# A mixture-of-experts tail where TensorE, not GpSimd, adds the two expert results of each token

## The chip, the cores and the metric

The kernel runs on one core of one Trainium2 chip. The metric is the device time of one execution in microseconds (us). Three executions of the kernel before took 910.62, 911.58 and 914.34 us (median 911.58). All data is float32 and one core does all the work.

## What is computed

Input x is 8 sequences of 1024 tokens of 128 numbers. Two blocks follow each other, each with a residual and a layernorm around it: a Mamba-2 mixer with a small MLP, and a mixture of 8 experts, of which each token takes two. Only the end of the second block matters here:

```python
probs = jax.nn.softmax(x @ Wr + br, axis=-1)
gates, ids = jax.lax.top_k(probs, K)                       # K = 2
...
h = jax.nn.silu(jnp.einsum('ecd,edh->ech', xg, W1) + b1[:, None, :])
out = jnp.einsum('ech,ehd->ecd', h, W2) + b2[:, None, :]
gated = out * disp_g.reshape(E, cap, 1)
y = jnp.zeros((N, Dm), x.dtype).at[disp_tok].add(gated.reshape(E * cap, Dm))
...
x = x + _layernorm(_L0_ffn_ref(...), axis=-1)
```

So every token has up to two gated expert results. They are added, the sum is normalised over its 128 numbers, and x (after the first block) is added.

## The kernel before

The program is written engine by engine; each engine has its own instruction list and they meet at semaphores (`need(engine, sem, t)` waits until step t of a producer is done, and its last argument allows so many steps of lead). Stages follow one another: normalisation, the mixer, the MLP, routing, and the last stage, in which the experts run and the results are combined. The change touches only that last stage.

**Experts.** 80 columns of 128 slots are cut into 24 pieces of 2 to 4 columns. For each piece GpSimd issues indirect DMAs that fetch the token rows (`fetch`, L1863), TensorE turns them (`turn`, L1888), multiplies them into `pH` (`up`, L1897, four banks) and `pO` (`down`, L1905), and turns them back into `pB` (`back`, L1913). ScalarE applies silu (L1928) and the output bias (L1935), VectorE scales by the gate (`results`, L1977), and GpSimd issues the indirect DMAs (`leave`, L1871) that scatter the rows into the DRAM tensor `choice`, first choices in its one half, second choices in the other. All eight PSUM banks belong to this stage: `pT` two, `pH` four, `pO` and `pB` one each.

**Combining.** When all scatters have landed, the 64 tiles of 128 tokens are gone through in 19 groups: 14 of 4 tiles, three of 2, two of 1 (`widths`). SyncE's queue loads for each group the first results into `ys` (L1846) and the second into `yb` (L1847), both SBUF; nine groups are loaded ahead, and from then on each store of group g (L1851) stands in front of the loads of group g+9. GpSimd waits for both loads and adds yb to ys in place (`both`, L1879). Then:

- VectorE, `moments` (L1985): one bn_stats for each tile of the sum;
- VectorE, `combined` (L1991): one bn_aggr for each tile;
- ScalarE, `rooted` (L1944): the square root of the variances;
- VectorE, `inverse` (L1997 and L1999): reciprocal and shift;
- ScalarE, `normal` (L1950): scale and shift, one activation for each tile, ys in place;
- VectorE, `add_x1` (L2004): one add of x over the group; then the store.

The order on VectorE is written out by hand: in iteration g it does moments of g, inverse of g-1, combined of g and add_x1 of g-2. ScalarE does the root of g and then the normalisation of g-1.

```python
in_turn(GROUPS, [(0, moments), (1, inverse), (0, combined), (2, add_x1)])   # VectorE
in_turn(GROUPS, [(0, rooted), (1, normal)])                                 # ScalarE
in_turn(GROUPS, [(0, load), (8, store)])                                    # SyncE
```

TensorE has nothing to do once the experts' last piece is turned back. At the kernel's start (L326, in `idle`) and at the start of the MLP (L1346) it is given products of ones with zeros that nobody reads.

Of the kernel before, what the change touches and what calls it, by code (L numbers as in the profile page):

```python
# [27 lines left out]
ALU = mybir.AluOpType  # L28
ACT = mybir.ActivationFunctionType
# [3 lines left out]
SEQS, LEN, D = 8, 1024, 128  # L33
# [25 lines left out]
def need(eng, sem, t, back=0):  # L59

    value = t + 1 - back
    if not isinstance(value, int) or value > 0:
        eng.wait_ge(sem, value)
# [33 lines left out]
def build(nc, x, ln_w, ln_b, in_proj_w, conv_w, conv_b, dt_bias, A_log, D_skip, rms_w, out_proj_w,  # L97
# [4 lines left out]
    with ExitStack() as ctx:  # L102
# [8 lines left out]
        def sem(name):  # L111
            s = nc.alloc_semaphore(name=name)
            stage_sems.append(s)
            return s
# [8 lines left out]
        ident = sb("ident", [P, P])  # L123
        ones = sb("ones", [P, P])
# [4 lines left out]
        zrow = sb("zrow", [P, 8 * D])  # L129
# [45 lines left out]
        with ExitStack() as st:  # L175
# [5 lines left out]
            def pst(name, shape):  # L181
                return st.enter_context(nc.psum_tensor(name, shape, F32))
# [18 lines left out]
            pT = [pst(f"n_pT{k}", [P, 2, 512]) for k in range(2)]  # L201
# [934 lines left out]
        with ExitStack() as st:  # L1136
            st.callback(stage_over)
            NB, G = 4, 2
            GROUPS, N = TILES // G, G * P
# [602 lines left out]
        with ExitStack() as st:  # L1742
# [4 lines left out]
            TOTAL = len(sizes)  # L1747
# [42 lines left out]
            def of_group(g):  # L1790
                return slice(first_tile[g], first_tile[g + 1])
# [5 lines left out]
            def in_turn(steps, stages):  # L1797

                for i in range(steps + max(lag for lag, _ in stages)):
                    for lag, stage in stages:  # L1800
                        if 0 <= i - lag < steps:
                            stage(i - lag)
            pT = [pst("e_pT0"), pst("e_pT1")]
            pH = [pst(f"e_pH{c}") for c in range(NF)]
            pO, pB = pst("e_pO"), pst("e_pB")
            s_we = [sem("e_we0"), sem("e_we1")]
            s_xg = [sem(f"e_xg{k}") for k in range(RING)]
            s_scat = [sem(f"e_scat{k}") for k in range(RING)]
# [46 lines left out]
            @block.gpsimd  # L1855
            def _(g):
                def fetch(n):
                    need(g, s_pt, n, RING)
                    need(g, s_g1, n, RING)
                    need(g, s_g2, n, RING)  # L1860
                    for i in range(sizes[n]):
                        c = starts[n] + i
                        g.indirect_dma_start(xg[:, n % RING, i, :], None, table,  # L1863
                                             bass.IndirectOffsetOnAxis(ap=token_of[:, c:c + 1], axis=0),
                                             bounds_check=TOKENS - 1, oob_is_err=False).then_inc(s_xg[n % RING], 16)

                def leave(n):
                    need(g, s_yo, n)
                    for i in range(sizes[n]):
                        c = starts[n] + i  # L1870
                        g.indirect_dma_start(choice, bass.IndirectOffsetOnAxis(ap=choice_of[:, c:c + 1], axis=0),  # L1871
                                             yo[:, n % RING, i, :], None, bounds_check=2 * TOKENS - 1,
                                             oob_is_err=False).then_inc(s_scat[n % RING], 16)
                g.wait_ge(filled, 16 * FILLS)
                staged([(0, fetch), (LAG, leave)])

                def both(n):
                    g.wait_ge(s_in[n], 32)
                    g.tensor_tensor(ys[:, of_group(n)], ys[:, of_group(n)], yb[:, of_group(n)], ALU.add).then_inc(s_ys2, 1)  # L1879
                in_turn(GROUPS, [(0, both)])  # L1880

            @block.tensor
            def _(pe):
                def turn(n):
# [32 lines left out]
                pe.wait_ge(s_bias, 1)  # L1917
                staged([(2, up), (3, down), (4, back), (0, turn)])

            @block.scalar  # L1920
            def _(a):
                def silus(n):
                    need(a, s_po, n, 2)
                    w = P * sizes[n]
                    for c in range(NF):
                        f = NF * expert(n) + c
                        need(a, s_ph, NF * n + c)
                        a.activation(hb[:, n % 2, c, 0:w], pH[c][:, 0:w], ACT.Silu, bias=bcols[:, f:f + 1]).then_inc(s_h, 1)  # L1928

                def outs(n):  # L1930
                    need(a, s_po, n)
                    need(a, s_pb, n, 2)
                    w = P * sizes[n]
                    f = EXPERTS * NF + expert(n)
                    a.activation(oT[:, n % 2, 0:w], pO[:, 0:w], ACT.Identity, bias=bcols[:, f:f + 1]).then_inc(s_o, 1)  # L1935
                a.wait_ge(s_turned, 1)
                a.activation(bcols[:, :], pB[:, 0:NR], ACT.Copy).then_inc(s_bias, 1)
                a.wait_ge(s_bias, 1)
                staged([(2, silus), (3, outs)])

                def rooted(g):
                    need(a, s_var, g)
                    w = widths[g]
                    a.activation(c_sd[:, g, 0:w], c_mv[:, g, 0:w, 1], ACT.Sqrt, bias=eps[:, 0:1]).then_inc(s_sd, 1)  # L1944

                def normal(g):
                    need(a, s_sh, g)
                    for i in range(widths[g]):
                        t = first_tile[g] + i
                        ins = a.activation(ys[:, t, :], ys[:, t, :], ACT.Identity, bias=c_sh[:, g, i:i + 1], scale=c_rs[:, g, i:i + 1])  # L1950
                    ins.then_inc(s_yna, 1)
                in_turn(GROUPS, [(0, rooted), (1, normal)])

            @block.vector
            def _(v):
                def gates_of(n):
                    k, w = n % RING, sizes[n]
                    arrived(v, n)
                    need(v, s_yo, n, RING)
                    v.tensor_tensor(g1[:, k, 0:w], xg[:, k, 0:w, D], is_first[:, columns(n)], ALU.mult).then_inc(s_g1, 1)  # L1960
                    v.tensor_tensor(g2[:, k, 0:w], xg[:, k, 0:w, D + 1], is_other[:, columns(n)], ALU.mult).then_inc(s_g2, 1)
                    need(v, s_g1, n)
                    need(v, s_g2, n)
                    v.tensor_tensor(gate[:, k, 0:w], g1[:, k, 0:w], g2[:, k, 0:w], ALU.add).then_inc(s_gate, 1)

                def fetched(n):
                    need(v, s_pt, n)
                    need(v, s_ph, NF * n + NF - 1, 3 * NF)
                    v.tensor_copy(xgT[:, n % 3, 0:P * sizes[n]], pT[n % 2][:, 0:P * sizes[n]]).then_inc(s_xgT, 1)  # L1969

                def results(n):
                    k, w = n % RING, sizes[n]
                    need(v, s_pb, n)
                    if n >= RING:
                        v.wait_ge(s_scat[k], 16 * blocks_upto(n - RING))
                    need(v, s_gate, n)
                    v.tensor_tensor(yo[:, k, 0:w, :], pB[:, 0:P * w].rearrange("p (i d) -> p i d", d=D),  # L1977
                                    gate[:, k, 0:w].unsqueeze(2).broadcast_to([P, w, D]), ALU.mult).then_inc(s_yo, 1)
                staged([(4, results), (0, fetched), (0, gates_of)])

                def moments(g):
                    need(v, s_var, g, 2)
                    need(v, s_ys2, g)
                    for i in range(widths[g]):
                        ins = v.bn_stats(c_st[:, g % 2, i, :], ys[:, first_tile[g] + i, :])  # L1985
                    ins.then_inc(s_st, 1)

                def combined(g):
                    need(v, s_st, g)
                    for i in range(widths[g]):  # L1990
                        ins = v.bn_aggr(c_mv[:, g, i, :], c_st[:, g % 2, i, :])  # L1991
                    ins.then_inc(s_var, 1)

                def inverse(g):
                    need(v, s_sd, g)
                    w = widths[g]
                    v.reciprocal(c_rs[:, g, 0:w], c_sd[:, g, 0:w]).then_inc(s_rs, 1)  # L1997
                    need(v, s_rs, g)
                    v.scalar_tensor_tensor(out=c_sh[:, g, 0:w], in0=c_mv[:, g, 0:w, 0], scalar=-1.0, in1=c_rs[:, g, 0:w],  # L1999
                                           op0=ALU.mult, op1=ALU.mult).then_inc(s_sh, 1)  # L2000

                def add_x1(g):
                    need(v, s_yna, g)
                    v.tensor_tensor(ys[:, of_group(g)], ys[:, of_group(g)], x1[:, of_group(g), :], ALU.add).then_inc(s_ot, 1)  # L2004
                in_turn(GROUPS, [(0, moments), (1, inverse), (0, combined), (2, add_x1)])


# [22 lines left out]
```

## Time and profile before

| | |
|---|---|
| median of three runs (lowest, highest) | 911.58 us (910.62, 914.34) |
| the profiled execution's own time | 916.2 us |
| its span, first to last instruction | 914.5 us |
| mean granted TensorE clock | 0.847 of full |
| TensorE / VectorE / ScalarE / GpSimd busy | 686.5 / 611.7 / 490.2 / 463.9 us |
| first load of the combining issued | 865.09 us into the span |

The times in rows of the trace are microseconds from the span's start. The median is the number to compare with; durations come from the one profiled execution. A granted clock of 1.00 is TensorE at 2.4 GHz, 0.50 at 1.2 GHz.

### The profile page before, as it was taken

How to read it: one execution, taken by the hardware profiler on the slowest of the kernel's cores; microseconds unless marked ns; L12 is line 12 of the kernel's file. 1: busy time of each engine (PE TensorE's matmuls, PEld its weight loads, DVE VectorE, ACT ScalarE, POOL GpSimd, SP SyncE). 2: the span in 40 equal slices, each digit the busy share in tenths (PEclk: the TensorE clock that was granted, in tenths of full speed). 3: DMA queues.
4: the chain of work that ended last, by engine and by line, in shares of the span. 5: the costliest groups of instructions: out<-in, count | busy, mean ns of one | idle time of the engine just before them, and what ended most of it. 6: DMA issues, size and time to landing. Idle time of an engine off the chain costs nothing. (4 is left out here: it accounts for less than half of the span.)

```text
span 914.5 us, 14429 instructions
## 1 busy us (share of the span) xinstructions
PE 686.5 (75%) x3774; PEld 479.3 (52%) x3774; DVE 611.7 (67%) x2161; ACT 490.2 (54%) x1207; POOL 463.9 (51%) x594
## 2 busy tenths in 40 slices
PE   7558999999999997999998311374977877888200
PEld 3325677777777765989897211242434433444100
DVE  7957999999999955899898687891111111111088
ACT  4874666667667765878775145151422332234157
POOL 7514676667666762334333500006567666765572
PEclk8867999999999999999999555555999878898755
DMA  8930000000000006000000040003212221221295
GB/s 211 394 115 1 1 1 2 1 1 2 1 2 1 1 2 170 16 2 1 2 1 1 1 187 0 0 0 89 60 40 72 67 62 42 72 65 39 69 347 171
DMA packets 50413, 52.91 MB, mean 58 GB/s; under 512 B 7576, under 2 KB 39624, under 8 KB 50080
## 3 DMA queue, kind: packets, MB, share of 16 engines
q1 hardware_dynamic: 44496, 41.62, 14.0%
q0 software_dynamic: 5120, 10.37, 4.3%
q8 instruction: 29, 0.48, 0.2%
q14 instruction: 48, 0.39, 0.2%
q10 hardware_dynamic: 720, 0.05, 0.1%
HBM read 28.04 MB, written 24.18 MB: 57 GB/s over the span
## 5 line engine op out<-in xcount | busy, mean ns | idle before, releaser
L888 DVE SCALAR_TENSOR_TENSOR s_cv<-s_pU,tap_w,s_cv 128x256 f32<-128x256 f32 x372 | 153.5, 477 | 12.3 <-ACT s_cv L819 12.0
L1863 POOL DMA_INDIRECT arena<-token_rows,token_of x80 | 81.3, 1017 | 118.3 <-issue 118.0
L1977 DVE TENSOR_TENSOR arena<-e_pB,e_gate 128x384 f32<-128x384 f32 (+2 forms) x24 | 14.5, 603 | 151.7 <-remote 106.4
L1871 POOL DMA_INDIRECT choice_rows<-arena,choice_of x80 | 79.6, 996 | 58.4 <-DVE arena L1977 37.0
L1928 ACT ACTIVATE e_h<-e_pH,e_bcols 128x384 f32<-128x384 f32 (+2 forms) x96 | 56.5, 618 | 91.6 <-remote 59.0
L1897 PE MATMUL e_pH<-e_xgT,e_w 128*128 128x384 f32 (+2 forms) x192 | 90.5, 605 | 14.7 <-issue 13.8
L1905 PE MATMUL e_pO<-e_h,e_w 128*128 128x384 f32 (+2 forms) x192 | 80.7, 568 | 7.9 <-ACT e_oT L1935 6.4
L687 POOL TENSOR_TENSOR s_xa<-s_xt,arena 128x512 f32<-128x512 f32 x32 | 34.4, 1076 | 88.4 <-ACT s_xt L837 88.4
L819 ACT ACTIVATE s_cv<-s_pU,tap_b,tap_w 128x256 f32<-128x256 f32 x124 | 63.7, 561 | 23.4 <-PE s_pU L721 23.0
L721 PE MATMUL s_pU<-arena,w_in 128*128 128x262 f32 x248 | 69.3, 403 | 7.7 <-DVE s_cv L888 3.4
L1905 PEld LDWEIGHTS e_pO<-e_h,e_w 128*128 128x128 f32 x192 | 39.7, 210 | 47.7 <-issue 37.1
L1897 PEld LDWEIGHTS e_pH<-e_xgT,e_w 128*128 128x128 f32 x192 | 36.9, 212 | 51.7 <-issue 37.4
L1370 PE MATMUL m_pM<-w_m,m_h 128*128 128x128 f32 x512 | 63.9, 279 | 0.1
L1361 PE MATMUL m_pH<-m_hT,w_m 128*128 128x256 f32 x256 | 60.7, 380 | 2.1 <-ACT m_h L1244 1.5
L1370 PEld LDWEIGHTS m_pM<-w_m,m_h 128*128 128x128 f32 x512 | 61.2, 196 | 0.3 <-issue 0.3
L1205 POOL TENSOR_TENSOR arena<-arena,m_un 128x256 f32<-128x256 f32 (+1 forms) x32 | 22.5, 702 | 65.0 <-DVE m_un L1280 65.0
L721 PEld LDWEIGHTS s_pU<-arena,w_in 128*128 128x128 f32 x248 | 43.0, 197 | 17.0 <-DVE s_cv L888 7.5
L1244 ACT ACTIVATE m_h<-m_pH,b_col 128x256 f32<-128x256 f32 x128 | 50.2, 484 | 0.0
L1361 PEld LDWEIGHTS m_pH<-m_hT,w_m 128*128 128x128 f32 x256 | 46.2, 190 | 7.5 <-ACT m_hT L1237 2.6
L1969 DVE COPY e_xgT<-e_pT 128x384 f32<-128x384 f32 (+2 forms) x24 | 14.3, 597 | 46.8 <-remote 30.7
L1935 ACT ACTIVATE e_oT<-e_pO,e_bcols 128x384 f32<-128x384 f32 (+2 forms) x24 | 14.8, 617 | 57.2 <-PE e_pO L1905 38.8
L699 POOL TENSOR_TENSOR s_y<-s_y,s_dx 128x512 f32<-128x512 f32 x32 | 40.9, 1277 | 4.9 <-DVE s_y L921 4.8
(293 smaller groups left out, 1846.7 us busy)
## 6 DMA issues: line engine op xcount, KB each, us to landing
choice_rows<-zrow SPq DMA_DIRECT2D x16, 512.0 KB, 6.8
arena<-choice_rows SPq DMA_DIRECT2D x28, 256.0 KB, 4.7
token_rows<-arena SPq DMA_DIRECT2D x8, 520.0 KB, 5.8
n_x<-in_L_attn_x_dram SPq DMA_DIRECT2D x8, 512.0 KB, 7.6
arena<-in_L_attn_x_dram SPq DMA_DIRECT2D x8, 512.0 KB, 4.6
e_w<-in_L_ffn_W_dram SPq DMA_DIRECT2D x16, 256.0 KB
out_dram<-arena SPq DMA_DIRECT2D x14, 256.0 KB, 2.5
decay_rows<-arena SPq DMA_DIRECT2D x2, 1024.0 KB, 4.7
```

What stands on the lines that cost most here:

```text
L699: g.tensor_tensor(y2[:, :], y1[:, p % 2, :], dx[:, p % 4, :], ALU.add).then_inc(s_y2, 1)
L721: pe.matmul(pU[m % 2][:, 0:G2 * XBLK], w_in[:, P * m:P * (m + 1)], xT[:, G2 * p:G2 * (p + 1), :].rearrange("p t c -> p (t c)"), start=True ...
L819: a.activation(by_tile(cv[:, p % 2, m, :]), columns(m)[:, :, 0:P], ACT.Identity, bias=tap_b[:, m:m + 1], scale=tap_w[:, m, 0:1]).then_inc( ...
L888: v.scalar_tensor_tensor(out=by_tile(cv[:, p % 2, m, :]), in0=columns(m)[:, :, tap:tap + P], scalar=tap_w[:, m, tap:tap + 1], in1=by_tile( ...
L1244: ins = a.activation(h1[:, m % NB, c, :], pH[half_][:, N * (c % 2):N * (c % 2 + 1)], ACT.Relu, bias=b1_col[:, c:c + 1])
L1361: ins = pe.matmul(pH[half_][:, N * c:N * (c + 1)], w_m1[:, P * f:P * (f + 1)], hT[:, m % NB, :], start=True, stop=True)
L1370: ins = pe.matmul(pM[m % 2][:, P * i:P * (i + 1)], h1[:, m % NB, c, P * i:P * (i + 1)], w_m2[:, c, :], start=(c == 0), stop=(c == NF - 1))
L1863: g.indirect_dma_start(xg[:, n % RING, i, :], None, table, bass.IndirectOffsetOnAxis(ap=token_of[:, c:c + 1], axis=0), bounds_check=TOKENS ...
L1871: g.indirect_dma_start(choice, bass.IndirectOffsetOnAxis(ap=choice_of[:, c:c + 1], axis=0), yo[:, n % RING, i, :], None, bounds_check=2 * ...
L1897: pe.matmul(pH[c][:, 0:w], we1[:, expert(n) % 2, P * c:P * (c + 1)], xgT[:, n % 3, 0:w], start=True, stop=True).then_inc(s_ph, 1)
L1905: ins = pe.matmul(pO[:, 0:w], we2[:, expert(n) % 2, c, :], hb[:, n % 2, c, 0:w], start=(c == 0), stop=(c == NF - 1))
L1928: a.activation(hb[:, n % 2, c, 0:w], pH[c][:, 0:w], ACT.Silu, bias=bcols[:, f:f + 1]).then_inc(s_h, 1)
```

## The change

Four banks of `pH`, the two of `pT`, `pO` and `pB` become a ring of eight, one bank for a group. TensorE first runs 18 products that nobody reads, then waits for the two loads of a group and multiplies `ys` and `yb` by the identity, one after the other, accumulating in the group's bank. GpSimd's add is gone. VectorE's bn_stats and ScalarE's normalising activation read the sum from the bank; the activation still writes ys in SBUF, where x is added to it. From the ninth group on TensorE also waits until the group eight earlier has been normalised (s_yna).

```diff
@@ -1803,6 +1803,11 @@
             pT = [pst("e_pT0"), pst("e_pT1")]
             pH = [pst(f"e_pH{c}") for c in range(NF)]
             pO, pB = pst("e_pO"), pst("e_pB")
+            banks = pT + pH + [pO, pB]
+            BANKS = len(banks)
+
+            def summed(g):
+                return banks[g % BANKS][:, 0:D * widths[g]]
             s_we = [sem("e_we0"), sem("e_we1")]
             s_xg = [sem(f"e_xg{k}") for k in range(RING)]
             s_scat = [sem(f"e_scat{k}") for k in range(RING)]
@@ -1874,11 +1879,6 @@
                 g.wait_ge(filled, 16 * FILLS)
                 staged([(0, fetch), (LAG, leave)])
 
-                def both(n):
-                    g.wait_ge(s_in[n], 32)
-                    g.tensor_tensor(ys[:, of_group(n)], ys[:, of_group(n)], yb[:, of_group(n)], ALU.add).then_inc(s_ys2, 1)
-                in_turn(GROUPS, [(0, both)])
-
             @block.tensor
             def _(pe):
                 def turn(n):
@@ -1917,6 +1917,18 @@
                 pe.wait_ge(s_bias, 1)
                 staged([(2, up), (3, down), (4, back), (0, turn)])
 
+                need(pe, s_xgT, TOTAL - 1)
+                for _ in range(18):
+                    pe.matmul(pT[0][:, :], ones[:, :], zrow[:, 0:512], start=True, stop=True)
+
+                def both(g):
+                    pe.wait_ge(s_in[g], 32)
+                    need(pe, s_yna, g, BANKS)
+                    for f, first in ((ys, True), (yb, False)):
+                        ins = pe.matmul(summed(g), ident[:, :], f[:, of_group(g)].rearrange("p t d -> p (t d)"), start=first, stop=not first)
+                    ins.then_inc(s_ys2, 1)
+                in_turn(GROUPS, [(0, both)])
+
             @block.scalar
             def _(a):
                 def silus(n):
@@ -1947,7 +1959,7 @@
                     need(a, s_sh, g)
                     for i in range(widths[g]):
                         t = first_tile[g] + i
-                        ins = a.activation(ys[:, t, :], ys[:, t, :], ACT.Identity, bias=c_sh[:, g, i:i + 1], scale=c_rs[:, g, i:i + 1])
+                        ins = a.activation(ys[:, t, :], summed(g)[:, D * i:D * (i + 1)], ACT.Identity, bias=c_sh[:, g, i:i + 1], scale=c_rs[:, g, i:i + 1])
                     ins.then_inc(s_yna, 1)
                 in_turn(GROUPS, [(0, rooted), (1, normal)])
 
@@ -1982,7 +1994,7 @@
                     need(v, s_var, g, 2)
                     need(v, s_ys2, g)
                     for i in range(widths[g]):
-                        ins = v.bn_stats(c_st[:, g % 2, i, :], ys[:, first_tile[g] + i, :])
+                        ins = v.bn_stats(c_st[:, g % 2, i, :], summed(g)[:, D * i:D * (i + 1)])
                     ins.then_inc(s_st, 1)
 
                 def combined(g):
```

On TensorE's instruction list, at the end of the experts, the built program shows this (one product is one row entry here; the names are those of the banks, and `arena` holds ys and yb):

```order
 L1905 MATMUL e_pO<-e_h,e_w 128x256 x4
 L1913 MATMUL e_pB<-ident,e_oT 128x128 x6
+L1922 MATMUL e_pT<-zrow,ones 128x512 x18
+L1928 MATMUL e_pT<-arena,ident 128x512 x4
+L1928 MATMUL e_pH<-arena,ident 128x512 x8
+L1928 MATMUL e_pO<-arena,ident 128x512 x2
+L1928 MATMUL e_pB<-arena,ident 128x512 x2
+L1928 MATMUL e_pT<-arena,ident 128x512 x4
+L1928 MATMUL e_pH<-arena,ident 128x512 x8
+L1928 MATMUL e_pO<-arena,ident 128x256 x2
```

The products of the combining stand behind the whole of the experts' work and behind the 18; nothing ahead of them has moved.

## Rows read from the trace of the kernel before

**Rows 1.** Page: TensorE's granted clock, in tenths, in 40 slices of the span.
```profile
PEclk8867999999999999999999555555999878898755
```

**Rows 2.** Stretches: length; PE, PEld, DVE, ACT, POOL busy; clock, DMA share, GB/s.
```profile
770.00:780.00 10.00, 7.90 (x19) 4.31 (x20) 2.36 (x7) 3.68 (x7) 4.72 (x5) 0.66 0.15 36
...
835.00:853.80 18.80, 17.49 (x63) 9.98 (x61) 3.13 (x8) 8.77 (x15) 11.22 (x13) 1.00 0.11 37
...
871.40:882.40 11.00, 0.00 (x0) 0.00 (x0) 9.04 (x43) 6.32 (x19) 10.71 (x8) 0.50 1.05 376
882.40:894.00 11.60, 0.00 (x0) 0.00 (x0) 11.43 (x56) 8.37 (x24) 6.68 (x7) 0.50 0.98 316
```

**Rows 3.** Timeline, groups 0 to 3 (start, us, instruction, idle before).
```profile
868.57 1.26 POOL L1879 TENSOR_TENSOR arena<-arena 128x512 f32<-128x512 f32 x1 [4.77 <-DMA arena<-choice_rows]
869.86 0.87 DVE L1985 BATCH_NORM_STATS2 c_stats<-arena 128x6 f32<-128x128 f32 x4 [15.57 <-POOL arena L1879]
...
871.40 11.04 POOL L1879 TENSOR_TENSOR arena<-arena 128x512 f32<-128x512 f32 x8 [1.57 <-DMA arena<-choice_rows]
...
877.12 0.86 DVE L1985 BATCH_NORM_STATS2 c_stats<-arena 128x6 f32<-128x128 f32 x4
```

**Rows 4.** Timeline, an iteration with GpSimd's add beside it.
```profile
880.02 0.86 DVE L1985 BATCH_NORM_STATS2 c_stats<-arena 128x6 f32<-128x128 f32 x4
...
881.45 1.54 DVE L2004 TENSOR_TENSOR arena<-arena 128x512 f32<-128x512 f32 x1
...
882.80 1.30 POOL L1879 TENSOR_TENSOR arena<-arena 128x512 f32<-128x512 f32 x1 [0.37 <-DMA arena<-choice_rows]
882.91 0.86 DVE L1985 BATCH_NORM_STATS2 c_stats<-arena 128x6 f32<-128x128 f32 x4
```

**Rows 5.** Timeline, VectorE from group 12's iteration on; groups 14 and 18.
```profile
899.20 0.86 DVE L1985 BATCH_NORM_STATS2 c_stats<-arena 128x6 f32<-128x128 f32 x4
...
900.54 0.74 DVE L2004 TENSOR_TENSOR arena<-arena 128x512 f32<-128x512 f32 x1
900.66 0.30 ACT L1944 ACTIVATE c_sd<-c_mv,eps 128x4 f32<-128x4 f32 x1 [0.36 <-DVE c_mv L1991]
900.86 1.63 ACT L1950 ACTIVATE arena<-arena,c_shift,c_rs 128x128 f32<-128x128 f32 x4
901.20 0.86 DVE L1985 BATCH_NORM_STATS2 c_stats<-arena 128x6 f32<-128x128 f32 x4
...
903.25 0.47 DVE L1985 BATCH_NORM_STATS2 c_stats<-arena 128x6 f32<-128x128 f32 x2
...
909.23 0.29 DVE L1985 BATCH_NORM_STATS2 c_stats<-arena 128x6 f32<-128x128 f32 x1
```

**Rows 6.** Timeline of TensorE at the end of the experts.
```profile
845.68 3.60 PE L1905 MATMUL e_pO<-e_h,e_w 128*128 128x512 f32 x8
...
853.42 0.41 PE L1913 MATMUL e_pB<-ident,e_oT 128*128 128x128 f32 x2 [0.87 <-DVE arena L1977]
```

**Rows 7.** Unread products at the start: timeline, and by line (ns min/median/max).
```profile
2.12 10.51 PE L326 MATMUL n_pE<-zrow,ones 128*128 128x512 f32 x18 [2.12 <-POOL zrow L269]
...
L326 PE MATMUL n_pE<-zrow,ones x18: 592/592/1194, 2.1 to 12.0; 128*128 128x512 f32 x18
```

**Rows 8.** Timeline, VectorE reading PSUM (s_pU), and SBUF only.
```profile
140.00 2.46 DVE L888 SCALAR_TENSOR_TENSOR s_cv<-s_pU,tap_w,s_cv 128x256 f32<-128x256 f32 x6
...
401.00 0.60 DVE L1300 SCALAR_TENSOR_TENSOR m_h<-arena,m_rooty,m_res 128x128 f32<-128x128 f32 x2
```

**Rows 9.** Groups of instructions (busy us, mean ns): these two kinds, another at two widths.
```profile
L888 DVE SCALAR_TENSOR_TENSOR s_cv<-s_pU,tap_w,s_cv 128x256 f32<-128x256 f32 x372 | 153.5, 477 | 12.3 <-ACT s_cv L819 12.0
...
L1300 DVE SCALAR_TENSOR_TENSOR m_h<-arena,m_rooty,m_res 128x128 f32<-128x128 f32 x64 | 22.0, 383 | 5.7 <-ACT m_res L1231 5.5
...
L1977 DVE TENSOR_TENSOR arena<-e_pB,e_gate 128x512 f32<-128x512 f32 x10 | 6.9, 692 | 84.3 <-remote 70.8 <-PE e_pB L1913 13.5
L1977 DVE TENSOR_TENSOR arena<-e_pB,e_gate 128x384 f32<-128x384 f32 x12 | 6.7, 558 | 64.8 <-remote 35.6 <-issue 16.2 <-PE e_pB L1913 12.9
```

## Prediction before the run

> **What bounds the kernel now.** I read the page first, for its line of granted clock: two of the last three slices stand at 5 tenths, in the stage in which TensorE has nothing to do [rows 1]. Only the combining is changed, from the first load at 865.09 us to the end, some 49 us of 914.5. The stretches inside it come next: VectorE is busy 9.04 of 11.00 us and then 11.43 of 11.60, GpSimd 10.71 and then 6.68 [rows 2]. GpSimd is full only until 882.4; from then on it waits for loads and VectorE is what is full. Last the timeline. GpSimd's add of group 0 starts when its loads land at 868.57, that of group 1 at 871.40, and eight follow in 11.04 us, 1.38 us each; VectorE's moments start at 869.86 for group 0 and at 877.12 for group 3 [rows 3]. From group 3 on VectorE never waits long, so its iteration, from one bn_stats of four to the next, is the length of the kernel here. It has two lengths. From 880.02 to 882.91 it took 2.89 us, and its last piece, the add of x, 1.54 us [rows 4]; with next to no GpSimd add beside it, from 899.20 to 901.20, it took 2.00 and that add about 0.66 (901.20 less 900.54) [rows 5]. The difference of 0.88 us is the time for which VectorE's two-input add stands still while GpSimd's add runs. Group 14's moments start at 903.25 [rows 5]: from group 3 to 14 there are 11 iterations in 26.13 us, 2.38 us each. ScalarE is close behind: its four activations take 1.63 us.
>
> **The change, part by part.** The sum is made against the profiled execution (span 914.5, own time 916.2 us) and the difference is then taken from the median of 911.58, which is 4.6 us lower.
>
> *GpSimd's add goes.* At 2.00 instead of 2.38 us, 11 iterations save 26.13 - 22.0 = 4.1 us. GpSimd has nothing else there, so this is all that it gives.
>
> *The 18 unread products.* A float32 product of 512 columns is two passes on TensorE. Eight passes of that shape took 3.60 us in the warm stretch before 853.8 (clock 1.00) [rows 2, 6]; with 0.59 for one pass alone [rows 7] the pitch is (3.60 - 0.59) / 7 = 0.43 us. The last turning-back ends at 853.42 + 0.41 = 853.83 [rows 6]. So the 36 passes run until 853.83 + 36 x 0.43 = 869.3, 0.7 us after group 0's loads have landed. They lie beside the last scatters and the first loads; only this 0.7 sticks out, and it is hidden unless it reaches group 3.
>
> *The identity products.* Two products, four passes, 1.72 us for a group of four tiles at full clock, where GpSimd took 1.3 to 1.4. A pass's result is complete 0.59 - 0.43 = 0.16 us after its pitch is over. Group 0: 869.3 + 1.72 + 0.16 = 871.2 (moments before: 869.86). Group 1: 871.4 + 1.88 = 873.3. Group 2 follows at once: 875.0. VectorE's iteration of group 2 then ends, with 2.2 us (next item), at 877.2, against 877.12 before. The late start thus costs 0.1 us by group 3. From there TensorE, at 1.72 us a group, runs ahead of VectorE, and its waits for a free bank (eight groups of lead) and for loads don't reach VectorE: group 9's loads, which are issued behind the store of group 0, land at 882.80 [rows 4], and their moments are not due before 890. Nine groups of loads ahead are also enough for the transfers: an iteration moves 786 KB (two loads, one store), which in 2.2 us is 357 GB/s, and 376 GB/s were moved between 871.4 and 882.4 [rows 2]. If only the 316 of the next stretch were to be had, 2.49 us an iteration, the 7 us of lead would be used up by 0.3 us a group, too slowly to matter.
>
> *VectorE reads the sum from PSUM.* No row of before has bn_stats on PSUM. From below: nothing, 4 x 0 us. From above: the taps read PSUM, six instructions of 256 columns in 2.46 us, pitch (2.46 - 0.48) / 5 = 0.40, of which 256 columns are 0.27, so 0.13 us are overhead; an instruction of the same kind on SBUF alone, 128 columns, two in 0.60, has a pitch of 0.22, less 0.13 for its columns, so 0.08 [rows 8] (0.48 and 0.38 us are what one of each takes; a column is (692 - 558) / 128 = 1.05 ns [rows 9]). PSUM costs about 0.05 us an instruction. Even if bn_stats, whose pitch is (0.86 - 0.27) / 3 = 0.196, 0.06 of it overhead [rows 5], rose to all of 0.13 and a little more, it would be 0.1 each. I take 0.05: it is the same engine with the same kind of source. Four make 0.2 us: the iteration is 2.2 instead of 2.0.
>
> The Trainium skill, "VectorE: DVE Perf Modes", in its section on the TRN2 errata, speaks against this part: a VectorE instruction has a fixed cost of 58 cycles on an SBUF source and of 120 on a PSUM one, at 0.96 GHz. By it, and this is an estimate from that page, each bn_stats would be 0.065 us dearer, the iteration 2.26 us, and the sum below would be 0.9 instead of 1.6 us. No row here shows bn_stats at either.
>
> *ScalarE reads from PSUM too.* An activation of 128 columns takes 0.41 us of ScalarE in rows of four (1.63 / 4) [rows 5]. I cost the move at nothing: with the root, at most 0.3 us more [rows 5], ScalarE needs at most 1.9 us a group, and VectorE's 2.2 covers it. If each were 0.07 us slower, 2.2 would just be met.
>
> *Sum.* Group 14's moments: 877.2 + 11 x 2.2 = 901.4 instead of 903.25, a gain of 1.85. In the last five, small groups eight bn_stats remain on the way, 8 x 0.05 = 0.4, of which I keep 0.2, since VectorE waits there for ScalarE anyway. Gain 1.6 us: span 912.9, own time 914.6, and for the median **911.58 - 1.6 = 910.0 us**. With PSUM at nothing the iteration is 2.0 and the gain 4.1 us: 907.5. With 0.1 us each it is 2.4: group 14 at 877.4 + 26.4 = 903.8, 0.55 late, and 0.4 behind it: 912.5.
>
> **Rivals.**
>
> *TensorE becomes the bound, because its clock falls.* At half clock a pass takes twice as long (the unread products at the start had 1.194 against 0.592 us, their first against their usual one [rows 7]), so a group of four takes 3.44 us. TensorE decides as soon as a group's four passes need more than VectorE's 2.2 us, at a mean clock under 0.78. At half clock throughout, from 869.3: 14 x 3.44 + 3 x 1.72 + 2 x 0.86 = 55.0, the last sum at 924.4; the kernel before needed 914.5 - 909.2 = 5.3 us from the last group's moments on [rows 5], so the span would be 929.7, 15.2 us longer: **926.8 us, slower**. For it: in the experts' stage the clock had a mean of 0.66 in a stretch of 10 us in which TensorE was busy for 7.90, work at half clock counted in [rows 2]. Against it: from 835 to 853.8, busy 17.49 of 18.80, it stayed at 1.00 [rows 2], and here TensorE has next to no gap from 854 until about 894, when only the small groups are left and even half clock (1.72 us for two tiles) is hidden.
>
> *The unread products don't do what they are for, or end too late.* If the first six of the 36 passes ran at half clock, as at the kernel's start, where 18 passes took 10.5 us instead of 18 x 0.43 + 0.16 = 7.9 [rows 7], 2.6 us would be added: first sum at 873.8, TensorE one group after the other, group 3 at about 879.4 instead of 877.2, all later ones 2.2 later: **912.2 us**. Against it: before 853.8 the engine is warm [rows 2].
>
> *A PSUM read costs VectorE nothing here*, because bn_stats hides it in its own pipeline. Then the full lock-out is gained: **907.5 us**. For it: bn_stats takes only 0.06 us more than its columns, less than any other instruction of these rows. Against: the taps' 0.05.
>
> **How the numbers follow.** A difference of 0.5%, 4.6 us, is about what a measurement of this kernel can tell from none. My forecast, 909 to 912.5, has 0.60. The fallen clock has 0.08, the late start 0.09, the free PSUM read 0.18; 0.05 is left for what I don't see, on either side. Faster by over 0.5% needs 4.6 us, more than all of the lock-out: a third of the free read's chance and half of the unseen, 0.09. Slower by over 0.5%: the fallen clock and a little of the rest, 0.10. Within 0.5%: 0.81. The range reaches over the free read and the late start, with an error of measurement of 1 to 2 us on either side: 906.0 to 914.5 us.
>
> **What would show it.** In the profile after: no GpSimd instruction in the combining; adds of x all near 0.66 us and none of 1.5; bn_stats of four in about 1.06 instead of 0.86 us; iterations of 2.2 us from group 3 to 13; the first identity product at about 869.3 us; TensorE's clock at 1.00 until about 894; VectorE never waiting for TensorE after group 2. I am wrong if the iterations are longer than 2.4 us, if VectorE waits for an identity product after group 3, or if the clock in that stretch is under 0.8.

## The result, and the profile after

Four runs of the changed kernel took 902.08 to 906.03 us, median **904.6 us**; four of the kernel before, 910.62 to 914.34, median 911.44. The ratio is 0.9921, with a 95% interval of 0.9893 to 0.995. Forecast were 910.0 us and a range of 906.0 to 914.5. The direction was right, the size was not: 6.8 us instead of 1.6.

The profiled execution took 906.03 us, its span is 904.3, where the one before had 914.5. In that trace two things are shorter. The page's clock line, now, with what stands against it in [rows 1]:

```profile
span 904.3 us, 14645 instructions
...
PEclk9867999999999999999999555555989888969998
```

The last three slices are at 9, 9 and 8 instead of 7, 5 and 5: TensorE keeps its clock to the end of the work that it was given.

SyncE's queue, the first load of the combining (start us, us, queue and line, transfer), from the timeline of after:

```profile
859.11 0.33 SPq L1851 DMA_DIRECT2D arena<-choice_rows  x1
```

It was at 865.09 before. So the **combining** took 904.3 - 859.1 = 45.2 us instead of 49.4, 4.2 less, and the stages ahead of it 6.0 us less, although nothing in them was changed. Of these 6.0, 5.3 lie in the experts' stage, from the first indirect fetch to the first load of the combining: 239.46 us against 244.72. The first is the change; what the second is, the experiments had to tell.

TensorE in the timeline of after (start, us, line, product, idle before; an ellipsis stands for rows left out, here and below):

```profile
847.47 0.41 PE L1913 MATMUL e_pB<-ident,e_oT 128*128 128x128 f32 x2 [0.88 <-DVE arena L1989]
847.72 15.62 PE L1922 MATMUL e_pT<-zrow,ones 128*128 128x512 f32 x36
863.17 1.88 PE L1928 MATMUL e_pT<-arena,ident 128*128 128x512 f32 x4
866.15 1.98 PE L1928 MATMUL e_pT<-arena,ident 128*128 128x512 f32 x4 [1.11 <-DMA arena<-choice_rows]
867.98 7.03 PE L1928 MATMUL e_pH<-arena,ident 128*128 128x512 f32 x16
```

36 unread passes take 15.62 us, a group of four identity passes 1.72 (the next start is 1.72 later where nothing is waited for: 16 passes in 7.03 less 0.16), group 0 starts 4.06 us after its first load was issued. Stretches of after, cut as those of [rows 2] but moved 6.3 us earlier (length; PE, PEld, DVE, ACT, POOL busy; clock, DMA share, GB/s):

```profile
865.10:876.10 11.00, 9.95 (x23) 4.48 (x24) 8.71 (x53) 6.04 (x19) 0.00 (x0) 1.00 1.03 372
876.10:887.70 11.60, 11.53 (x27) 4.77 (x26) 11.40 (x67) 10.08 (x31) 0.00 (x0) 1.00 1.06 341
887.70:897.70 10.00, 6.11 (x24) 3.54 (x22) 9.39 (x54) 8.70 (x27) 0.00 (x0) 1.00 0.76 231
```

GpSimd is at zero. TensorE's clock is 1.00 in all three. VectorE is as full as before, and in the second stretch it runs 67 instructions in the time in which 56 ran before.

One iteration of VectorE, with ScalarE between, from the timeline of after:

```profile
881.70 0.89 DVE L1997 BATCH_NORM_STATS2 c_stats<-e_pT 128x6 f32<-128x128 f32 x4
882.50 0.17 DVE L2009 RECIPROCAL c_rs<-c_sd 128x4 f32<-128x4 f32 x1
882.70 0.16 DVE L2011 SCALAR_TENSOR_TENSOR c_shift<-c_mv,c_rs 128x4 f32<-128x4 f32 x1
882.78 0.37 DVE L2003 BATCH_NORM_AGGREGATE c_mv<-c_stats 128x2 f32<-128x6 f32 x4
883.07 0.66 DVE L2016 TENSOR_TENSOR arena<-arena 128x512 f32<-128x512 f32 x1
...
883.39 1.48 ACT L1962 ACTIVATE arena<-e_pB,c_shift,c_rs 128x128 f32<-128x128 f32 x4
883.65 0.88 DVE L1997 BATCH_NORM_STATS2 c_stats<-e_pT 128x6 f32<-128x128 f32 x4
```

881.70 to 883.65 is 1.95 us. From group 3 to group 14 all eleven iterations are 1.94 or 1.95, 21.35 us together; it was 26.13, with 2.00 for the quietest that I had looked at [rows 5] and 2.89 for those beside a GpSimd add [rows 4]. The add of x takes 0.66 us each time in these iterations. Four bn_stats on PSUM take 0.89 instead of 0.86, and the four activations 1.48 instead of 1.63. I had predicted iterations of 2.2.

### The profile page after: what moved, and what is told of

Same layout as the page of the kernel before. It is cut to its first block and busy times, and to the rows that moved or that the text cites. A ratio compares the mean times of both kernels' runs of the same rounds, so it can differ in the third digit from the quotient of the medians.

```text
span 904.3 us, 14645 instructions
## 1 busy us (share of the span) xinstructions
PE 724.1 (80%) x3886; PEld 496.4 (55%) x3886; DVE 606.5 (67%) x2161; ACT 486.9 (54%) x1207; POOL 441.2 (49%) x575
## 5 line engine op out<-in xcount | busy, mean ns | idle before, releaser
L1897 PE MATMUL e_pH<-e_xgT,e_w 128*128 128x384 f32 (+2 forms) x192 | 86.1, 591 | 13.6 <-ACT e_h L1940 11.6
L1905 PE MATMUL e_pO<-e_h,e_w 128*128 128x384 f32 (+2 forms) x192 | 78.5, 554 | 13.1 <-ACT e_oT L1947 11.1
L1361 PEld LDWEIGHTS m_pH<-m_hT,w_m 128*128 128x128 f32 x256 | 46.2, 190 | 7.5 <-ACT m_hT L1237 2.6
```

The costliest lines, as they stand in the source:

```text
L1361: ins = pe.matmul(pH[half_][:, N * c:N * (c + 1)], w_m1[:, P * f:P * (f + 1)], hT[:, m % NB, :], start=True, stop=True)
L1897: pe.matmul(pH[c][:, 0:w], we1[:, expert(n) % 2, P * c:P * (c + 1)], xgT[:, n % 3, 0:w], start=True, stop=True).then_inc(s_ph, 1)
L1905: ins = pe.matmul(pO[:, 0:w], we2[:, expert(n) % 2, c, :], hb[:, n % 2, c, 0:w], start=(c == 0), stop=(c == NF - 1))
```

## The experiments

Two theories on the 6.8 us, named as in the expectations below. *Scatter*: the combining gives some 4 us, and the rest is the length of the experts' stage, which differs from execution to execution. *Upstream gain*: the changed kernel makes the experts' stage shorter as well. And three questions inside the combining: is it GpSimd's lock-out that went (VectorE's two-input instructions standing still while GpSimd's add runs), what do the PSUM sources cost, and what do the unread products do? "Combining" is always the span less the start of the first load of the results, in one trace. All ratios are to the kernel before on the same chip.

**The kernel before, again.** No edit.

> The kernel before, unchanged, for a second trace and its scatter. Theory 'scatter': the experts' stage (first indirect fetch to first load of the combining), 244.7 us in the first trace against 239.5 in the changed kernel's, varies from execution to execution by some us, so this trace's will differ from 244.7 by 1 to 5 us either way, and the combining stays at 49.4 us. Theory 'upstream gain': the stage is 244 to 245 us again, and the changed kernel's is shorter each time.

Twelve runs, 906.69 to 916.6 us, median 911.3; ratio 1.0009 (0.9982 to 1.0036). One run scatters with a standard deviation of 2.85 us. Combining 48.8 us (first load at 863.87, span 912.7), experts' stage 244.4.

**The changed kernel, again.** No edit.

> The changed kernel, unchanged, with more rounds. Combining 45.2 us as in the first trace (4.2 less than before). Theory 'scatter': median 4 us under the kernel before's, ratio about 0.9955, and the experts' stage somewhere in 238 to 246 us. Theory 'upstream gain': median 6.5 to 7 us under, ratio about 0.992, experts' stage at or under 240 us.

Twelve runs, median 906.48, ratio 0.995 (0.9926 to 0.9974), that is 4.9 us. Combining 45.1 us, experts' stage 242.2 where the first trace had 239.5. That is 'scatter' by the median, and the experts' stage is over the 240 of 'upstream gain'.

**The kernel before with 18 unread products.**

```diff
                 staged([(2, up), (3, down), (4, back), (0, turn)])
+                need(pe, s_xgT, TOTAL - 1)
+                for _ in range(18):
+                    pe.matmul(pT[0][:, :], ones[:, :], zrow[:, 0:512], start=True, stop=True)
```

> The kernel before with only the 18 unread products added behind the experts' work; GpSimd still adds. If the combining alone was changed by the change, this is 911.4 us, within 1 us: the products wait for nobody and nobody waits for them. Under the theory 'upstream gain', in which TensorE's longer program or the products themselves change something before the combining, it is 2 to 3 us faster than the kernel before.

Median 911.16 of 12, ratio 1.0007 (0.9979 to 1.0036), no effect to be seen. Its trace has an experts' stage of 239.9 us, as short as that of the changed kernel's first trace, and no change that could account for it; the combining took 47.9 us. Over all thirteen traces of this study the experts' stage took 239.5 to 248.4 us, the 248.4 in a version of the changed kernel. The ratio's interval allows a gain of at most 1.9 us, less than the 2 to 3 us of 'upstream gain'. So the 5.3 us ahead of the combining in the first pair of traces are within the scatter, and need no effect of the change; an effect of under 2 us is not excluded.

**The changed kernel without the unread products.**

```diff
-                need(pe, s_xgT, TOTAL - 1)
-                for _ in range(18):
-                    pe.matmul(pT[0][:, :], ones[:, :], zrow[:, 0:512], start=True, stop=True)
```

> The changed kernel without the 18 unread products. TensorE idles for some 15 us and its clock is at half when group 0 lands. Theory 'the unread products hold the clock': the first groups take 3.44 us each; if the identity products then bring the clock back after some us of full work, TensorE is late by 2 to 5 us for a few groups and catches up at 1.72 against 1.94 us an iteration only slowly, so the end is 1 to 4 us later than the changed kernel's, 906 to 909 us. If the clock stays at half throughout: some 15 us later. Rival 'they are not needed': the same time as the changed kernel or 1 us less, since group 0 is then not held up.

Median 907.55 of 12, ratio 0.9971 (0.9945 to 0.9998), 1.1 us over the changed kernel; combining 45.8 against 45.1. Stretches of its trace, before and after its first identity product at 863.25 (columns as above):

```profile
848.50:863.20 14.70, 0.01 (x1) 0.00 (x0) 0.42 (x1) 0.10 (x1) 7.84 (x8) 0.59 0.28 86
863.25:869.30 6.05, 6.05 (x9) 2.56 (x10) 1.27 (x8) 0.30 (x1) 0.00 (x0) 0.59 0.94 321
869.30:890.00 20.70, 20.70 (x50) 9.22 (x49) 19.84 (x117) 16.91 (x50) 0.00 (x0) 1.00 1.06 360
```

In the 14.7 idle us the clock has fallen, to 0.50 in their last four, from 859 to 863. Its mean is 0.59 over the first 6 us of the identity products, and then it is 1.00 by itself. The first moments come 7.3 us after the first load instead of 6.0, and from group 3 on the iterations are 1.94 us again. So in this pair of traces the 18 unread products are worth 0.7 us of the combining, and without them the fallen clock costs about a twentieth of the 15.2 us that I had priced for it: it came back while the identity products ran. The unread products also have a price. The first identity product starts 3.49 us after the first load without them and 4.06 with them, behind the last of them.

**The kernel before, GpSimd's add left out** (only the first choice's rows are normalised):

```diff
-                    g.tensor_tensor(ys[:, of_group(n)], ys[:, of_group(n)], yb[:, of_group(n)], ALU.add).then_inc(s_ys2, 1)
+                    g.sem_inc(s_ys2, 1)
```

> The kernel before with GpSimd's add left out: it waits for the loads and signals, so only the first choice's rows are normalised; everything else is as before, bn_stats on SBUF. Theory 'lock-out': the combining's gain is the removal of GpSimd's adds, so here too all adds of x take 0.66 us, the iteration is 1.9 to 1.95 us, and the combining is 44 to 45 us (49.4 before). If the 2.00 us of the prediction were the undisturbed length, it is 2.00. Rival 'TensorE or PSUM brings the gain': iterations stay at 2.4 us in the mean and the combining at 48 to 49 us.

This kernel, those with bn_stats on SBUF and with an unread GpSimd add beside, and the first with the add of x on GpSimd ran on a second chip, where the kernel before had a median of 916.69. Median 909.33 of 6, ratio 0.9917 (0.9885 to 0.9949). The combining took 42.7 us, less than expected, since group 0's moments start 3.5 us after the first load instead of 4.8. The iterations are not 2.00 but alternate, 1.92 and 2.02. Two of them, from the timeline (L1985 the moments, L2004 the add of x, L1950 the normalisation):

```profile
888.45 0.86 DVE L1985 BATCH_NORM_STATS2 c_stats<-arena 128x6 f32<-128x128 f32 x4
...
889.79 0.67 DVE L2004 TENSOR_TENSOR arena<-arena 128x512 f32<-128x512 f32 x1
...
890.11 1.63 ACT L1950 ACTIVATE arena<-arena,c_shift,c_rs 128x128 f32<-128x128 f32 x4
...
890.37 0.86 DVE L1985 BATCH_NORM_STATS2 c_stats<-arena 128x6 f32<-128x128 f32 x4
...
891.43 0.37 DVE L1991 BATCH_NORM_AGGREGATE c_mv<-c_stats 128x2 f32<-128x6 f32 x4
891.77 0.69 DVE L2004 TENSOR_TENSOR arena<-arena 128x512 f32<-128x512 f32 x1
892.39 0.86 DVE L1985 BATCH_NORM_STATS2 c_stats<-arena 128x6 f32<-128x128 f32 x4
```

In the first, the add of x starts at once. In the second it starts at 891.77, 0.34 us after the start of the aggregates instead of 0.29, when ScalarE's four activations, started at 890.11, are over (891.74). So the undisturbed iteration is 1.92 us, and ScalarE, at 1.63 for four, adds 0.1 to every second one. With the lock-out gone the eleven iterations come to 21.6 us (11 x 1.97) against 26.13. That is nearly all of what the changed kernel gains there (21.35), without TensorE and without PSUM; the changed kernel's combining is longer than this one's because its first moments come 2.5 us later (6.0 after the first load).

**The changed kernel, bn_stats on SBUF** (its moments are the first choice's alone):

```diff
-                        ins = v.bn_stats(c_st[:, g % 2, i, :], summed(g)[:, D * i:D * (i + 1)])
+                        ins = v.bn_stats(c_st[:, g % 2, i, :], ys[:, first_tile[g] + i, :])
```

> The changed kernel with bn_stats reading ys in SBUF (the first choice's rows alone, so the moments are not those of the sum); all waits are kept. If a PSUM source costs bn_stats 0.05 us each, as predicted, the iteration is 0.2 us shorter than the changed kernel's 1.94, 1.74 us, and the kernel 2.5 us faster than it; by 0.065 each, 1.68 us. If it costs nothing in a row of four, 1.92 to 1.94 us and the same time.

Iterations of 1.92 us throughout, combining 44.9 us; median 912.16 of 12, ratio 0.996 (0.9934 to 0.9986), not to be told from the changed kernel's 0.995. From its timeline:

```profile
889.82 0.86 DVE L1997 BATCH_NORM_STATS2 c_stats<-arena 128x6 f32<-128x128 f32 x4
890.60 0.16 DVE L2009 RECIPROCAL c_rs<-c_sd 128x4 f32<-128x4 f32 x1
```

The reciprocal starts 0.78 us after the first of the four, and 0.80 in the changed kernel. PSUM costs bn_stats 0.02 us for four, 0.005 each, a tenth of what I took. The Trainium skill, "VectorE: DVE Perf Modes", in its section on the TRN2 errata, gives 58 cycles of fixed cost on SBUF and 120 on PSUM, 0.065 us more each; for bn_stats in a row of four this trace disagrees, with 0.005, and it decides.

**The changed kernel, normalising from SBUF** (the first choice's rows, with the sum's moments):

```diff
-                        ins = a.activation(ys[:, t, :], summed(g)[:, D * i:D * (i + 1)], ACT.Identity, bias=c_sh[:, g, i:i + 1], scale=c_rs[:, g, i:i + 1])
+                        ins = a.activation(ys[:, t, :], ys[:, t, :], ACT.Identity, bias=c_sh[:, g, i:i + 1], scale=c_rs[:, g, i:i + 1])
```

> The changed kernel with ScalarE's normalising activations reading ys in SBUF (the first choice's rows instead of the sum); all waits are kept. If the PSUM source is what makes four of them 1.49 instead of 1.63 us, they are 1.63 again, VectorE's add of x waits for them in every second iteration as in the kernel before with the add left out, and the iterations alternate between 1.94 and 2.02 or 2.04 us; combining 45.7 us. If not, 1.94 throughout.

One run, 907.75 us, on a third chip, where the kernel before had a median of 911.96. Combining 46.2, 0.5 more than expected; part of that is the start, since group 3's moments came 13.1 us after the first load, and 12.9 and 12.5 in the first two traces of the changed kernel. The iterations alternate between 1.94 and 2.02 from group 3 on. From the timeline:

```profile
882.52 1.63 ACT L1962 ACTIVATE arena<-arena,c_shift,c_rs 128x128 f32<-128x128 f32 x4
...
883.85 0.37 DVE L2003 BATCH_NORM_AGGREGATE c_mv<-c_stats 128x2 f32<-128x6 f32 x4
884.19 0.69 DVE L2016 TENSOR_TENSOR arena<-arena 128x512 f32<-128x512 f32 x1
```

The activations are 1.63 us again and the add of x waits for them until 884.15. The PSUM source takes 0.035 us off each activation, and that is what makes the changed kernel's iterations even. The same section of the Trainium skill, "VectorE: DVE Perf Modes", gives ScalarE 224 cycles on SBUF and 172 on PSUM, 0.043 us less at 1.2 GHz; this trace, with 0.035, is close to it.

**The changed kernel with an unread GpSimd add beside:**

```diff
+                def beside(n):
+                    g.wait_ge(s_in[n], 32)
+                    need(g, s_ys2, n)
+                    need(g, s_aside, n, 1)
+                    g.tensor_tensor(aside[:, 0:widths[n]], yb[:, of_group(n)], yb[:, of_group(n)], ALU.add).then_inc(s_aside, 1)
+                in_turn(GROUPS, [(0, beside)])
```

> The changed kernel with an add on GpSimd for each group that nobody reads (yb plus yb into a buffer of its own, after the identity products of the group). Theory 'lock-out': VectorE's adds of x take up to 1.5 us again where they meet it, iterations of 2.4 us or more for some groups, combining 47 to 49 us instead of 45.2, 2 to 4 us slower than the changed kernel. Rival 'the gain came from GpSimd's latency in the chain, not from its use of SBUF': same as the changed kernel, 45.2 us.

Combining 46.8 us, 1.6 more than the changed kernel and just under the 47 to 49 expected; median 912.88 of 12, ratio 0.9961 (0.9934 to 0.9988), too coarse to show 1.6 us. The trace shows it. A long iteration, from 876.45 to 879.16, 2.71 us:

```profile
876.45 0.88 DVE L2006 BATCH_NORM_STATS2 c_stats<-e_pH 128x6 f32<-128x128 f32 x4
...
877.65 1.04 POOL L1888 TENSOR_TENSOR c_aside<-arena 128x512 f32<-128x512 f32 x1 [0.23 <-PE e_pH L1937]
877.81 1.43 DVE L2025 TENSOR_TENSOR arena<-arena 128x512 f32<-128x512 f32 x1
879.16 0.88 DVE L2006 BATCH_NORM_STATS2 c_stats<-e_pH 128x6 f32<-128x128 f32 x4
```

VectorE's add of x begins 0.16 us after GpSimd's add and ends at 879.24, GpSimd's end (878.69) plus 0.55. Two of the eleven iterations were of this kind (2.71 and 2.66 us), four more took 2.03 to 2.14; where the two don't meet, the iteration is 1.93 or 1.94. The eleven come to 23.3 us, between the changed kernel's 21.35 and the 26.13 of before: this add meets VectorE's less often. In the Trainium skill, "SBUF — State Buffer", section "Who interferes with whom", a VectorE instruction with two SBUF inputs contends with a GpSimd instruction that reads SBUF, and the contention is an exclusive lock; this trace agrees, with 1.43 us for an add of 0.66.

**The add of x on GpSimd.** If only VectorE's two-input instructions are locked out, VectorE can be cleared of them. The shift becomes one instruction a tile, and GpSimd adds x for groups 0 to 12; VectorE keeps 13 to 18:

```diff
-                    v.scalar_tensor_tensor(out=c_sh[:, g, 0:w], in0=c_mv[:, g, 0:w, 0], scalar=-1.0, in1=c_rs[:, g, 0:w],
-                                           op0=ALU.mult, op1=ALU.mult).then_inc(s_sh, 1)
+                    for i in range(w):
+                        ins = v.tensor_scalar(c_sh[:, g, i:i + 1], c_mv[:, g, i:i + 1, 0], c_rs[:, g, i:i + 1], -1.0, ALU.mult, ALU.mult)
+                    ins.then_inc(s_sh, 1)
...
+                def add_x1(n):
+                    need(g, s_yna, n)
+                    g.tensor_tensor(ys[:, of_group(n)], ys[:, of_group(n)], x1[:, of_group(n), :], ALU.add).then_inc(s_ot, 1)
```

> A version meant to beat both: the changed kernel with the add of x on GpSimd for the first 13 groups, and the shift on VectorE as one tensor_scalar a tile, whose scalars come by partition, instead of one two-input instruction, so that VectorE has nothing left that GpSimd's add can lock out. VectorE's iteration falls from 1.94 to about 1.65 us (0.66 less, 0.35 more for the shifts); ScalarE then needs 1.69 and TensorE 1.72, so 1.75 us. Thirteen iterations save 2.5 us: combining 42.7 us. Rival: the per-tile shifts or bn_stats are locked out too, or the stores come later by GpSimd's 1.3 us; then it is no faster than the changed kernel.

Iterations of 1.75 us, combining 43.0; median 908.12 of 7, ratio 0.9933 (0.9898 to 0.9967). From its timeline:

```profile
882.05 0.85 DVE L2003 BATCH_NORM_STATS2 c_stats<-e_pH 128x6 f32<-128x128 f32 x4
...
882.19 1.27 POOL L1885 TENSOR_TENSOR arena<-arena 128x512 f32<-128x512 f32 x1 [0.48 <-ACT arena L1968]
882.38 1.49 ACT L1968 ACTIVATE arena<-e_pT,c_shift,c_rs 128x128 f32<-128x128 f32 x4
882.83 0.16 DVE L2015 RECIPROCAL c_rs<-c_sd 128x4 f32<-128x4 f32 x1
883.02 0.58 DVE L2018 TENSOR_SCALAR c_shift<-c_mv,c_rs 128x1 f32<-128x1 f32 x4
```

GpSimd's add runs over VectorE's bn_stats, reciprocal and shifts, and none of them is longer for it: the four shifts take 0.58 us, as they did for group 0, before GpSimd's first add.

**The same with a semaphore of its own for VectorE's adds, and 17 unread products.**

> As the version with the add of x on GpSimd, but VectorE's own adds of the last six groups signal on a semaphore of their own and so don't wait for GpSimd's last one (0.9 us at group 15 there), and 17 unread products instead of 18, so that group 0's identity products start when its loads land. Combining 43.0 - 0.9 - 0.3 = 41.8 us, 3.4 us under the changed kernel's; median 3 to 3.5 us under it. Rival: with VectorE's wait gone the stores at the end are what is last, and it stays at 43 us.

This and the next ran on the third chip. Combining 44.1 us, not 41.8. Group 1's loads landed late in this execution (its moments came 3.4 us after group 0's; 1.95 in the trace before), which is 1.5 of the difference. The rest is my misreading of the 2.8 us iteration at group 15 of the trace before: it is there again, 2.7 us. From the timeline:

```profile
892.43 1.51 ACT L1972 ACTIVATE arena<-e_pH,c_shift,c_rs 128x128 f32<-128x128 f32 x4
...
893.97 0.69 DVE L2029 TENSOR_TENSOR arena<-arena 128x512 f32<-128x512 f32 x1 [0.70 <-ACT arena L1972]
```

VectorE's first add of x waits for ScalarE, not for GpSimd. Median 904.21 of 6, ratio 0.9931 (0.9905 to 0.9957).

**The changed kernel, a third time**, beside it:

> The changed kernel once more, on the same chip as its successor. Combining 45.1 to 45.2 us; ratio to the kernel before 0.995, as 12 runs gave, and not 0.992, as the first four.

Median 905.62 of 12, ratio 0.9948 (0.9925 to 0.9971), as expected; combining 44.5 us, 0.6 under what was expected. Its group 3 started 11.9 us after the first load, where the first trace had 12.9, since group 1's loads had landed after 6.1 us instead of 7.0. So the version with the add on GpSimd is 1.4 us under it in the median, with iterations 0.19 us shorter in both of its traces; the intervals overlap, and that it beats the changed kernel is shown for the iteration and not for the whole.

## Why the prediction was wrong

**What bounds the kernel.** Right: VectorE's iteration did, before and after, and the lock-out by GpSimd's add is what made it long. Leaving that add out, with nothing on TensorE, shortened it about as much (1.97 us in the mean); putting an unread one back lengthened it again, in six of eleven iterations.

**"At 2.00 instead of 2.38 us."** Wrong by 0.08. I took the quietest iteration of one trace for an undisturbed one. In [rows 5] the add of x shows 0.74 us, not 0.66: a small GpSimd add still touched it. It is in the trace of before:

```profile
900.27 0.45 POOL L1879 TENSOR_TENSOR arena<-arena 128x128 f32<-128x128 f32 x1 [1.55 <-DMA arena<-choice_rows]
```

It ends at 900.72, and VectorE's add at 901.28, 0.56 us later, as in the long iteration above. The undisturbed length is 1.92, and 0.1 more in every second iteration where ScalarE is late. I had the row and read the gap to the next start instead of the add's own length.

**The unread products and the identity products.** Right in price: 15.6 us for 36 passes (forecast 15.5), 1.72 for a group. Group 0's moments came 6.0 us after the first load (forecast 871.2 - 865.1 = 6.1), group 3's at 12.9. I had forecast 12.1, 0.1 later than before; it was 0.9 later, because group 1's loads landed 7.0 us after the first issue and not 6.3. TensorE stayed ahead of VectorE and its clock at 1.00, as argued.

**"PSUM costs about 0.05 us an instruction. ... Four make 0.2 us."** This is the step that failed. It measured 0.005, 0.02 for four. I carried a price over from two-input instructions with a semaphore each to single-input ones in a row; the lower bound, nothing, was nearly the value. Which of these differences makes the price small here, no run shows. Eleven iterations at 0.2 are 2.2 us, of which 0.2 were real.

**"ScalarE reads from PSUM too ... I cost the move at nothing."** It gained 0.035 us an activation, 0.14 a group, and so took away the 0.1 us that ScalarE had cost every second iteration, about 0.5 us in all.

**The sum.** For groups 3 to 14 I forecast 24.2 us where 26.13 were, and 21.35 were measured: 2.0 of the missed 2.85 us by the PSUM term, the rest by the iteration's length and by ScalarE. The combining thus gained 4.2 us in the first pair of traces, 3.8 from the mean of three traces of it before (48.7; 49.4, 48.8 and 47.9, the last with unread products) to three after (44.9). That is the rival "a PSUM read costs VectorE nothing here", 907.5 us, to which I had given 0.18. That its 4.1 us and the 4.2 of the first pair agree is partly luck: the eleven iterations gave 4.8 us, the later start took 0.9 of them back, and the small groups at the end gave 0.3.

**From the sum to the median.** The first four runs showed 6.8 us, below my range. With 12 runs each its median is 4.9 and, on another chip, 6.3 us under that of the kernel before. The ratios, 0.995 and 0.9948, stand for 4.6 and 4.7 us, and their intervals hold 3.8 us (0.9958) too. One run of this kernel scatters with a standard deviation of 2 to 3 us; in the traces most of it is in the experts' stage, and some ahead of it (the first indirect fetch starts between 617.1 and 621.4 us). Four runs against four therefore tell less than I allowed for when I added 1 to 2 us on either side. Whether what the medians show beyond the 3.8 us of the combining, 1.1 and 2.5 us and 3.0 in the first four runs, is more than scatter stays open: the experts' stage of nine traces of the changed kernel and its versions has a mean of 241.8 us, that of four traces of the kernel before and its versions 244.1, with single ones from 239.5 to 248.4 in the former and from 239.9 to 247.5 in the latter; both of the longest are from the second chip.

## What to carry to other kernels

Where two engines exclude each other, the quietest iteration of a trace is still not an undisturbed one; look at the length of each locked instruction in it, and take the shortest of each. A price for reading PSUM belongs to the kind of instruction it was measured on, and where no row has the kind in question, the bound "nothing" deserves as much as the neighbour's price. And before a small gain is judged, read the length of the stage that was changed in a few traces: here, over three traces each, it spread by 1.5 us before (47.9 to 49.4) and 0.7 after (44.5 to 45.2), and single iterations repeated to 0.01 us, where the whole spread by 6 us and more over 12 runs.

## What the runs showed of the hardware that was not expected

- Four bn_stats of 128 columns on PSUM took 0.80 us to the next instruction and on SBUF 0.78; four activations with scale and bias took 1.49 us from PSUM and 1.63 from SBUF.
- The unread GpSimd add of 512 columns (yb plus yb) took 1.04 us where VectorE was not in its way and up to 1.55 where it was: the exclusion works both ways.
- A tensor_scalar on VectorE with its scalars by partition was not held up by GpSimd's add (four in 0.58 us under it), where in the kernel before the two-input instruction for the same shift, L1999, had taken up to 0.83 us instead of 0.16 beside GpSimd's add:

```profile
890.26 1.26 POOL L1879 TENSOR_TENSOR arena<-arena 128x512 f32<-128x512 f32 x1 [1.00 <-DMA arena<-choice_rows]
...
890.71 0.83 DVE L1999 SCALAR_TENSOR_TENSOR c_shift<-c_mv,c_rs 128x4 f32<-128x4 f32 x1
```

- After 14.7 idle us and at a clock of 0.50, TensorE came back to 1.00 within the first 6 us of the identity products, without any unread ones.
